# A transformer kernel on one core: null-value product in one fp16 matmul, decay product in three fp16 passes with splits on GpSimd, and one home for two norm buffers

## The reference, cut to what matters

```python
x = x + tanh(g_xattn[0]) * cross_attention(layernorm(x), ctx)   # 16 heads of 64
x = x + tanh(g_ffn[0])   * quantized_ffn(layernorm(x))          # hidden 1024
x = x + tanh(g_xattn[1]) * depool(layernorm(x), ctx, boundaries)
x = x + tanh(g_ffn[1])   * mixture_of_experts(layernorm(x))     # 8 experts, 2 per token
```

## Time and profile before

| what | value |
|---|---|
| median of 3 runs | 1779.32 us (1778.08 to 1781.38) |
| the profiled execution, its own time | 1782.04 us |
| span of its profile | 1780.2 us |
| mean granted TensorE clock | 0.963 of full |
| PE busy | 1522.6 us, 86% of the span |
| DVE busy | 1202.0 us, 68% |
| ACT busy | 925.8 us, 52% |
| POOL busy | 592.0 us, 33% |

### The profile page before, as it was taken

One profiled execution on the slowest core, in us unless ns is written; L12 is line 12 of the kernel. 1 busy time (PEld: TensorE's weight loads), 2 busy tenths in 40 slices (PEclk: granted clock), 3 DMA queues, 4 the chain that ended last, 5 costly groups with the idle time before them and its releaser, 6 DMA issues. The chain is left out here.

```text
span 1780.2 us, 36819 instructions
## 1 busy us (share of the span) xinstructions
PE 1522.6 (86%) x12540; PEld 1084.8 (61%) x12541; DVE 1202.0 (68%) x3316; ACT 925.8 (52%) x2530; POOL 592.0 (33%) x777
## 2 busy tenths in 40 slices
PE   3899999999999999999999999986538887888784
PEld 2667676676766767667676776755425454555452
DVE  5478888788887888878888788886433433333332
ACT  4377676766767667676676766755112222222221
POOL 3002323233332333323333233332423444444442
PEclk9899999999999999999999999998759999999997
DMA  7101202021020210202102021031016222222224
GB/s 241 60 1 61 66 7 72 7 67 65 9 72 7 66 61 12 72 7 67 56 18 72 2 71 49 8 109 63 20 58 177 45 44 44 44 44 44 44 44 121
DMA packets 78142, 97.97 MB, mean 55 GB/s; under 512 B 20576, under 2 KB 61680, under 8 KB 77936
## 3 DMA queue, kind: packets, MB, share of 16 engines
q1 hardware_dynamic: 51152, 77.01, 13.6%
q0 software_dynamic: 15872, 18.95, 6.6%
q10 hardware_dynamic: 10976, 0.13, 0.3%
HBM read 65.02 MB, written 35.23 MB: 56 GB/s over the span
## 5 line engine op out<-in xcount | busy, mean ns | idle before, releaser
L801 ACT ACTIVATE prob<-S,nm 128x256 f32<-128x256 f32 x512 | 235.5, 474 | 81.8 <-issue 41.2
L794 ACT ACTIVATE pTh<-T 128x512 f16<-128x512 f32 x256 | 139.5, 597 | 136.0 <-PE T L975 135.8
L1303 PE MATMUL S<-GL,xgh 128*128 x576 | 173.8, 384 | 10.1 <-issue 8.8
L1494 DVE TENSOR_REDUCE mx<-S 128x2 f32<-128x512 f32 x256 | 163.3, 679 | 21.2 <-PE S L1048 20.7
L645 POOL TENSOR_SCALAR ve_ln<-mv_ln 128x2 f32<-128x2 f32 x64 | 14.7, 229 | 470.6 <-DVE mv_ln L1468 469.7
L1506 DVE SCALAR_TENSOR_TENSOR pTl<-T,pTh 128x512 f16<-128x512 f32 x256 | 164.1, 682 | 6.5 <-ACT pTh L794 6.5
L716 POOL DMA_INDIRECT xg<-x_rows,trow x72 | 70.4, 978 | 230.2 <-DMA acc_rows<-ysb,yid 99.3
L810 ACT ACTIVATE prob<-prob,rden 128x256 f32<-128x256 f32 x256 | 116.5, 504 | 56.5 <-DVE p0n L1515 55.8
L975 PE MATMUL T<-ident,prob 128*128 128x128 f32 x1024 | 142.2, 283 | 1.6 <-DVE prob L1519 1.4
L953 ACT ACTIVATE aH<-T 128x512 f16<-128x512 f32 x72 | 43.0, 597 | 192.0 <-PE T L975 144.4
L970 PE MATMUL W<-cTh,Wkh 128*128 128x256 f16 x512 | 140.3, 274 | 0.0
(11 more groups left out here) (296 smaller groups left out, 4457.3 us busy)
## 6 DMA issues: line engine op xcount, KB each, us to landing
cx<-in_ctx_dram SPq DMA_DIRECT2D x16, 512.0 KB
gst<-in_L_ffn_gating_w_dram SPq DMA_DIRECT2D x16, 512.0 KB
gating_split<-gsp SPq DMA_DIRECT2D x16, 512.0 KB
GL<-gating_split SPq DMA_DIRECT2D x8, 1024.0 KB
stg<-in_L_xattn_Wkv_dram SPq DMA_DIRECT2D x8, 512.0 KB, 13.5
xl<-in_x_dram SPq DMA_DIRECT2D x16, 256.0 KB
lst<-in_L_ffn_linear_w_dram SPq DMA_DIRECT2D x16, 256.0 KB
xres<-in_x_dram SPq DMA_DIRECT2D x16, 256.0 KB
```

What stands on the lines that cost most here:

```text
L794: A(flat(pTh[:, h, :, :]), T[h][:, :], ACT.Copy).then_inc(s_pTh[h], 1)
L801: ins = A(prob[:, h, t, :], S[h][:, t * NTOK:(t + 1) * NTOK], ACT.Exp, bias=nm[:, h, t:t + 1], scale=SM, accum_out=rs[:, h, t:t + 1])
L1303: ins = M(o[:, :], (xgl if n == 2 else xgh)[r % 2][:, k, :], GLflat[:, bass.ds(w, HID)], start=(k == 0 and n == 0), stop=(k == KD - 1 and ...
L1494: ins = V.tensor_reduce(mx[:, h, :], S[h][:, :].rearrange("p (t k) -> p t k", t=TT), AX.X, ALU.max)
```

## The change

- **Null values.** `p0n` gets 96 columns in place of 16: the same null probabilities three times, in columns 0 to 15, 32 to 47 and 64 to 79, the rest zero. The transposed tile `p0T` becomes fp16 with 96 rows: rows 0 and up hold the high part, rows 32 and up the low part, rows 64 and up the high part again. `Wnv` becomes fp16 with 96 rows: high, high, low. One fp16 matmul of 96 rows takes the place of the fp32 one. ACT copies all 96 rows, as before, but now only signals `half`; DVE then overwrites rows 32 to 47 with the low part, after `divide(0)`, and that instruction signals `free`.
- **Decay.** `dec` and `u` are split on GpSimd, each by a copy to fp16 and a subtraction of 128 x 512 elements. `dec` is split after `xb` and before the chain of `ln4`; `u` is split after that chain and before the work on `lst`. `win_unit` does three fp16 passes in place of each fp32 matmul, and waits for the splits (`s_gts`, `s_us`) in place of `s_gt` and `s_u`. There is one `u` in place of two; DVE waits before writing it for the last split.
- **Buffers.** `x4` is `xh`, and `x4T` is `xn`. DVE's wait for `s_x4o` moves from round 7 (before `ln4`) to round 2 (before `ln2`).
- **Setup.** GpSimd clears a `nvsel` of 768 columns in place of 128 and both `p0n`; DVE writes six sets of columns of `nvsel` in place of two, and a second instruction for the low rows of `Wnv`.

The diff, cut to its core:

```diff
-UNITS = [("p0T", False, POST), ("ctxT", True, PRE), ("ctxT", True, PRE), ("wout", False, POST),
+UNITS = [("p0T", True, POST), ("ctxT", True, PRE), ("ctxT", True, PRE), ("wout", False, POST),
...
+NULL_ROWS = 96
...
-        Wnv = sb("Wnv", [HEADS, D])
+        Wnv = sb("Wnv", [NULL_ROWS, D], FP16)
...
-        u = [sb(f"u{i}", [P, TT, D]) for i in range(2)]
+        u = sb("u", [P, TT, D])
+        uh, ul = [sb(f"uh{i}", [P, TT, D], FP16) for i in range(2)], [sb(f"ul{i}", [P, TT, D], FP16) for i in range(2)]
...
-        p0T = sb("p0T", [HEADS, NTOK])
+        p0T = sb("p0T", [NULL_ROWS, NTOK], FP16)
...
+        dech, decl = sb("dech", [P, 2, NTOK], FP16), sb("decl", [P, 2, NTOK], FP16)
         x3 = sb("x3", [P, TT, D])
-        x4 = sb("x4", [P, TT, D])
-        x4T = sb("x4T", [P, KD, NTOK])
+        x4 = xh
+        x4T = xn
...
# GpSimd, setup
+            for n in range(2):
+                link(pool.memset(p0n[n][:, :, :], 0.0))
...
# GpSimd, step
                     ins.then_inc(s_x2b, 1)
+                    wait_apart(pool, s_gt, post.n + 1)
+                    link(pool.tensor_copy(dech[:, :, :], dec[:, :, :]))
+                    pool.tensor_tensor(decl[:, :, :], dec[:, :, :], dech[:, :, :], ALU.subtract).then_inc(s_gts, 1)
                     rstd_of("ln4", post, 1e-5).then_inc(s_rstd["ln4"], 1)
                     wait_apart(pool, s_rstd["ln4"], post.n + 1)
                     rms_of_normed("ln4", 1e-6).then_inc(s_rms, 1)
+                if PRE in parts:
+                    wait_apart(pool, s_u, nxt.n + 1)
+                    link(pool.tensor_copy(uh[nxt.par][:, :, :], u[:, :, :]))
+                    pool.tensor_tensor(ul[nxt.par][:, :, :], u[:, :, :], uh[nxt.par][:, :, :], ALU.subtract)\
+                        .then_inc(s_us, 1)
                 if ATTN in parts:
...
# ScalarE, step, round 0; one_of is whole() with half[k] in place of free[k]
                     if j == 0 and post_:
-                        whole("p0T", p0T[:, :])
+                        one_of("p0T", p0T[:, :])
...
# TensorE, step
                     for t in range(TT):
-                        ins = tr(o[0:HEADS, t * P:(t + 1) * P], p0n[post.par][:, t, :])
+                        ins = tr(o[0:NULL_ROWS, t * P:(t + 1) * P], p0n[post.par][:, t, :])
...
                     evicted("xhT")
-                    pe.wait_ge(s_gt, post.n + 1)
-                    pe.wait_ge(s_u, post.n + 1)
+                    pe.wait_ge(s_gts, post.n + 1)
+                    pe.wait_ge(s_us, post.n + 1)
...
                         for k in range(2):
-                            ins = M(o[:, c], dec[:, k, tok], u[post.par][:, k, :], start=False, stop=(k == 1))
+                            ins = mm3(o[:, c], dech[:, k, tok], decl[:, k, tok], uh[post.par][:, k, :],
+                                      ul[post.par][:, k, :], False, k == 1)
...
# VectorE, setup
-            V.tensor_scalar(Wnv[:, :], banks_of[12][0:HEADS, 0:D], WS, None, ALU.mult).then_inc(s_init, 1)
+            link(V.tensor_scalar(Wnv[:, :], banks_of[12][0:NULL_ROWS, 0:D], WS, None, ALU.mult))
+            V.scalar_tensor_tensor(Wnv[64:64 + HEADS, :], banks_of[12][64:64 + HEADS, 0:D], WS, Wnv[64:64 + HEADS, :],
+                                   ALU.mult, ALU.subtract).then_inc(s_init, 1)
...
# VectorE, divide(j)
-                    V.tensor_tensor(p0n[i.par][:, :, 2 * j:2 * j + 2].rearrange("p t h -> p h t"), p0[:, :, :],
-                                    rden[:, :, :], ALU.mult).then_inc(s_rden, 1)
+                    V.tensor_tensor(p0n[i.par][:, :, :].rearrange("p t (r s) -> p r s t", s=32)[:, :, 2 * j:2 * j + 2, :],
+                                    p0[:, :, :].unsqueeze(1).broadcast_to([P, NULL_ROWS // 32, 2, TT]),
+                                    rden[:, :, :].unsqueeze(1).broadcast_to([P, NULL_ROWS // 32, 2, TT]),
+                                    ALU.mult).then_inc(s_rden, 1)
...
# VectorE, step
                     if j == 2 and post_:
+                        dve.wait_ge(s_x4o, 16 * (post.n + 1))
                         normed("ln2", post, xh, tiles(x1), rstd["ln2"]).then_inc(s_nrm["ln2"], 1)
...
                     if attn:
                         divide(j)
 
+                    if j == 0 and post_:
+                        k, _, nhalf = work.at["p0T"][0]
+                        dve.wait_ge(half[k], nhalf)
+                        V.scalar_tensor_tensor(p0T[32:32 + HEADS, :], W[k][32:32 + HEADS, 0:NTOK], 1.0,
+                                               p0T[32:32 + HEADS, :], ALU.mult, ALU.subtract).then_inc(free[k], 1)
                     if j == 0:
                         if pre:
                             low("ctxT", 0, flat(cTl[:, 0:2, :]), flat(cTh[:, 0:2, :]))
...
                     if j == 7:
                         if post_:
-                            dve.wait_ge(s_x4o, 16 * (post.n + 1))
                             normed("ln4", post, x4, tiles(x3), rstd["ln4"]).then_inc(s_nrm["ln4"], 1)
                         if pre:
                             dve.wait_ge(s_rstd["ctx"], nxt.n + 1)
+                            at_least(dve, s_us, nxt.n)
```

More of the change, by code:

```diff
@@ L154 @@
 POOL_CHUNKS = (4, 6)
-POOL_STEPS = 18
+POOL_STEPS = 20
 def build(nc, x, ctx, lens, g_xattn, g_ffn, Wq, Wkv, null_kv, Wout, ln_scale, ln_bias, w1, b1, w2, b2,
@@ L228, in build @@
         tokid = sb("tokid", [P, TT], I32)
+        p0n = [sb(f"p0n{i}", [P, TT, NULL_ROWS]) for i in range(2)]
         phase.append(ExitStack())
@@ L242, in build @@
         neg = sb("neg", [P, 2, NB])
-        nvsel = sb("nvsel", [P, KF, HEADS])
+        nvsel = sb("nvsel", [P, KF, NULL_ROWS])
         fillt = sb("fillt", [P, TABLE_COLS, 2], I32)
@@ L276, in build @@
         rden = sb("rden", [P, 2, TT])
-        p0n = [sb(f"p0n{i}", [P, TT, HEADS]) for i in range(2)]
-        p0T = sb("p0T", [HEADS, NTOK])
+        p0T = sb("p0T", [NULL_ROWS, NTOK], FP16)
         pTh, pTl = sb("pTh", [P, 2, 2, NTOK], FP16), sb("pTl", [P, 2, 2, NTOK], FP16)
@@ L396, in build @@
         s_ol = sem("attn_low")
-        s_u = sem("u_ready")
+        s_u, s_us = sem("u_ready"), sem("u_split")
         s_xb = sem("xres_biased")
@@ L403, in build @@
         s_dec = sem("decay_exp")
-        s_gt = sem("decay_ready")
+        s_gt, s_gts = sem("decay_ready"), sem("decay_split")
         s_ms = sem("experts_selected")
@@ L817, in whole, with one_of @@
                     A(dst, W[k][0:dst.shape[0], 0:dst.shape[1]], ACT.Copy).then_inc(free[k], 1)
+                def one_of(name, dst):
+                    k, nfull, _ = work.at[name][0]
+                    act.wait_ge(full[k], nfull)
+                    A(dst, W[k][0:dst.shape[0], 0:dst.shape[1]], ACT.Copy).then_inc(half[k], 1)
                 def q_high(m):
@@ L1016, in _ @@
             for f in range(KF):
-                ins = M(banks_of[12][0:HEADS, 0:D], nvsel[:, f, :], stg[CHUNKS - 2 + f // 4][:, (f % 4) * D:(f % 4 + 1) * D],
+                ins = M(banks_of[12][0:NULL_ROWS, 0:D], nvsel[:, f, :], stg[CHUNKS - 2 + f // 4][:, (f % 4) * D:(f % 4 + 1) * D],
                         start=(f == 0), stop=(f == KF - 1))
@@ L1377, in _ @@
             V.tensor_copy(lensT[:, :, :].rearrange("p a b -> p (a b)"), banks_of[1][:, 0:2 * NB]).then_inc(s_udve, 1)
[L1378 to L1381, removed]
+            every, last = NULL_ROWS + 2, (NULL_ROWS + 2) * (KF - 1) + 1
+            for part in range(2):
+                r = slice(64 * part, 64 * part + 64)
+                for at in range(part, NULL_ROWS, 32):
+                    ins = V.tensor_copy(nvsel[r, :, :].rearrange("p a b -> p (a b)")[:, at:at + last:every],
+                                        nvc[r, :].broadcast_to([64, KF]))
+            ins.then_inc(s_nvsel, 1)
             V.tensor_scalar(gres64[:, :], gresc[:, :], WS, None, ALU.mult).then_inc(s_udveg, 1)
@@ L1729, in step @@
                             dve.wait_ge(s_rstd["ctx"], nxt.n + 1)
+                            at_least(dve, s_us, nxt.n)
                             for t in range(TT):
-                                ins = V.scalar_tensor_tensor(u[nxt.par][:, t, :], cx[nxt.par][:, t, 0:D], rc[:, t:t + 1],
+                                ins = V.scalar_tensor_tensor(u[:, t, :], cx[nxt.par][:, t, 0:D], rc[:, t:t + 1],
                                                              gi_b[:, :], ALU.mult, ALU.mult)
```

## The result

The changed kernel takes 1870.29 us (median of 4 runs, 1864.65 to 1871.48) against 1780.35 for the kernel before on the same chips: a ratio of 1.0504, 95% interval 1.0481 to 1.0527. That is 90 us more, 12 above the forecast of 1858 and inside its range. The span of the profiled execution, the shortest of the four, is 1862.9 us.

The account below looks back on a forecast made before the run. PE was taken to set the pace of the steady batch steps, with DVE not far behind. Fifteen steps at +5.25 us, -1 for step 16 and +0.5 setup made +78.2 on 1779.3: 1858 us, range 1822 to 1888.

Parts of the forecast that it names:

- The wait, +6.0: Ahead of the output projection in round 0: PE idles 6.0 us a step for p0T's low half, behind `divide(0)` on DVE.
- The clock, +2.0: In the output projection: after the idle gap PE's clock falls to 1.2 GHz, costing 2.0 us a step.
- Rival 1: At the output projection: the stall comes but the clock stays at 2.4 GHz, giving 1828 us; chance 0.12.
- GpSimd under DVE's `select`, +0.5: In DVE's choice of experts: GpSimd's moved subtraction lies over `msel` and delays it, +0.5 us a step, bounds 0 and 1.16.
- Rival 2: At `msel`: GpSimd's subtraction blocks it fully, +1.16; 1868 us by contention alone, 1891 with other high bounds; chance 0.12.
- What is given back, -1.6: PE's waits after the projection (xn, pTl, xTl, part of hq) shrink as DVE catches up: -1.6 us a step.
- The products, -1.2 and -0.45: On PE: fp16 passes replacing fp32 shorten the null-value product by 1.2 and the decay product by 0.45 us a step.
- Rival 3: Head of round 0: p0T's low half is in time, only the products' gains remain, 1754 us; with rival 4, chance 0.08.
- Rival 4: In the steps: DVE, not PE, sets the pace and absorbs the stall, 1755 to 1783 us; with rival 3, chance 0.08.
- Buffers and setup: Shared buffers and the 12-element `p0n` cost nothing; setup's second instruction on `Wnv` costs 0.5 us once.
- The sum: Over steps 1 to 15: the terms add to +5.25 us each, +78.7; with step 16 and setup +78, giving 1858 us.

Follow-up runs that it names:

- e5: The changed kernel with GpSimd's split of u moved behind the ln2 chain of the next step: 1861.64 us, ratio 1.0435 to the kernel before.
- e4: The kernel before with only p0T's bank freed by a one-column DVE copy behind divide(0): 1872.16 us, ratio 1.0500.
- e2: The kernel of e5 with 46 unread matmuls put into PE's wait ahead of the output projection: 1831.87 us, ratio 1.0284 to the kernel before.
- e1: The changed kernel without DVE's instruction for p0T's low half, ACT freeing the bank: 1784.68 us, ratio 1.0028 to the kernel before.
- e8: The kernel of e1 with the split of u moved as in e5: 1774.46 us, ratio 0.9968 to the kernel before.
- e7: The kernel of e5 with the null-value product back to fp32, 16 rows, ACT freeing the bank: 1774.28 us, ratio 0.9966 to the kernel before.
- e9: The kernel before with the shared buffers alone: 1780.72 us, ratio 0.9998.
- e10: The kernel of e6 with GpSimd's four indirect DMAs moved into the next step, behind the rstd of ln1: 1778.02 us, ratio 0.9983 to the kernel before.
- e11: The kernel before with only the four indirect DMAs moved into the next step, behind the rstd of ln1: 1782.97 us, ratio 1.0003.
- e3: The kernel of e5 with DVE's instruction for p0T's low half moved ahead of maxima(0): 1784.01 us, ratio 1.0007 to the kernel before.
- e6: The kernel of e3 with DVE's low-half instruction ahead of `place` as well: 1789.86 us, ratio 1.0046 to the kernel before.
- e12: The kernel of e7 with the four indirect DMAs moved into the next step, behind the rstd of ln1: 1778.15 us, ratio 0.9988 to the kernel before.

## Why the prediction was right, point by point

- *The wait, +6.0.* Right in place, mechanism and size: e5 shows 6.06 us, and e4 shows that the wait alone makes the loss (1.0500 against 1.0504 for the whole change). In the changed kernel itself the idle time ahead of the projection is 4.91 in the step shown and 5.23 in the next, because PE gets there later over slow transposes; so the waits sum to 72.5 + 5.2 = 78 us and not to the 90 that I expected to see. Taken from the end of the values of round 7 to the start of the projection, the stretch has about 7.1 us more than before: from PE's wait for `msel`, (539.20 - 1.77) to 547.89, 10.5, against (510.46 - 0.92) to 512.93, 3.4. That is the 6.2 us that e5's steps have more at the same place, and 0.9 for `msel`.
- *The clock, +2.0.* Right: e2 against e5 gives 29.8 / 15 = 2.0 us. In the changed kernel the projection takes 8.18 and 7.09 us in turn, 7.55 on the mean of nine steps, against 5.56 at the full clock (e2): 2.0 again. Rival 1, that the clock stays up, fell.
- *GpSimd under DVE's `select`, +0.5.* Right mechanism, too small: `msel` went from 0.17 to 1.01 us, +0.84 in most steps; moving the split gave 9 us in one pair (changed kernel to e5) and 10 in another (e1 to e8), 0.6 to 0.7 a step. Rival 2's time for the contention alone, 1868, is nearer to the measured 1870 than my 1858. The Trainium skill's rule on the port shared by VectorE and GpSimd ("SBUF — State Buffer", "SBUF: two separate sides") has such an operation blocked for the rest of GpSimd's instruction; `msel` ended with the subtraction to 0.02 us, so the trace agrees. Its price of 1.16 would have been the bound; `msel` started 0.2 us after the subtraction. Not every pair agrees: `d`, a two-input operation of 128 x 4, started at 505.15 us in the changed kernel, 0.18 us into a GpSimd instruction with one input (`dec<-arg`, 1.50 us), and took 0.45 us in place of 0.15, so it was held up but not to that instruction's end.
- *What is given back, -1.6.* About right: the waits for xn, pTl and xTl are gone from the steady window (3.5, 8.2 and 4.7 us there before, some 1.8 a step together, where I had 1.2), but the wait for hq grew from 4.6 to 6.5 us where I had counted on 0.4 less a step.
- *The products, -1.2 and -0.45.* Right as lengths (6.69 against 5.56 us for the projection; for the decay product the 0.48 us a step that e7 waits longer for pTl), and behind the stall they count: from e4 to e5, the same stall without and with them, a step goes from 80.40 to 79.34 us although e5's wait is 0.35 longer. That they count because PE sets the pace of the steady steps was wrong where there is no stall: there e8, e7 and e9 have the same step to 0.04 us.
- *Rival 3, 1754 if p0T's low half is in time.* The step of it that failed is its price: it counted both products as gains in the case without a stall, 1.65 us a step. e8, e7 and e9 show that they are worth nothing there, since PE then waits for xn and pTl. The nearest thing to that rival is e8, 1774. I had used the trailing of DVE in round 1 in the forecast and left it out of the rival. Rival 4, that DVE rather than PE sets the step, was wrong for time added to PE and fits the runs for time taken from it.
- *Buffers and setup.* Buffers nothing (e9), `p0n` with 12 elements nothing (0.18 us against 0.17). The setup's 0.5 can't be told: the first p0T copy starts at 141.5 us against 140.9 before, but at 140.0 in e1 and 141.9 in e5, which have the same setup as the changed kernel.
- *The sum.* 5.25 us a step were forecast. Measured over nine steady steps it is 80.15 - 74.37 = 5.8: 7.1 in the stretch up to the projection where I had 6.5, 2.0 for the clock as forecast, less 1.1 and 0.45 for the products and less some 1.7 for what is given back. So the terms come out one by one, and not by errors that cancel; the stretch, `msel` above all, makes most of the 12 us by which the forecast was low.

Left open: why e10's waits for pTl hold as much as they do was read from the waits, not tested by moving DVE's work of round 0; why the moved DMAs make the waits for xh and pTl longer in e11 and e12; what holds the steady step at 74.3 us; and where the 7 us of e7 and e8 come from.

## What to carry to other kernels

When the release of a buffer moves from one engine to another, the price is not the instruction's length but its place in the new engine's queue: here 0.42 us of work, behind a chain through another engine, made a kernel 80 us slower, and four places further ahead nearly all of it was back (e5 to e3). Before shortening work on the busiest engine, look at its next waits: if another engine's result is already late there, the time saved turns into waiting, as 1.65 us a step did here. And look for the gain in the steps of the trace before you give a shorter run a cause. And moving work on GpSimd is not free for VectorE: look at which two-input operations of VectorE's critical chain it will lie over.

## What the runs showed of the hardware that was not expected

- Work that nobody reads made a kernel faster: 46 added matmuls a step, 5 us of PE time, took 29.8 us off (e5 to e2), by keeping the clock at its 2.4 GHz level.
- A wait of 1.77 us for `msel` was followed by a fall of the clock to the 1.2 GHz level in the changed kernel (0.82 in the window from 539 us, then slow transposes), and one of 1.95 us for xn in e6. In e1 the same wait of 1.77 us went both ways within one execution: in the step at 511 us the clock stayed up behind it, and from the step at 738 us on it fell in each step. Behind waits of 6 us it fell in every step of e5, where the mean clock over the projection is from 0.65 to 0.80. The two windows of e1:

```profile
511.00:512.00 1.00, 0.75 (x15) 0.69 (x17) 1.00 (x3) 0.00 (x0) 0.16 (x1) 1.00 0.00 0
738.00:739.00 1.00, 1.00 (x7) 1.00 (x6) 0.90 (x10) 0.38 (x1) 0.00 (x0) 0.50 1.00 401
```
- A 16-column operation of VectorE took between 176 and 1010 ns (`msel` in e1), with nothing changed but what GpSimd did beside it:

```profile
L1628 DVE TENSOR_TENSOR msel<-oh x16: 176/1008/1010, 210.0 to 1309.6; 128x16 f16<-128x16 f32 x16
```
